# Attention over the batch: row statistics on ScalarE instead of VectorE, and PSUM places that swap by tile

## The chip, the cores and the metric

The kernel runs on one core of a Trainium2 chip. The metric is the device time of one execution in microseconds; an execution that is profiled on the hardware gives the profile. The core has five engines with a queue each: TensorE (PE; its weight loads are PEld) for matrix products, VectorE (DVE), ScalarE (ACT) and GpSimd (POOL) for elementwise work, and SyncE (SP), which here issues transfers. Each queue runs in order; engines wait for each other only by counting semaphores.

## The reference, cut to what matters

The input `x` is 4 x 2048 rows of 256 values. Two layers follow; each normalises the rows, makes an attention-like sum `s` and a gate `g` and adds `s * silu(g)` to `x`. The changed code is the end of the first layer and the attention of the second:

```python
x = x + s * g                                  # end of layer 0
xn = _layernorm(x)                             # (x - mean) / sqrt(var + 1e-5), per row
q, k, v = xn @ Wq.T + bq, xn @ Wk.T + bk, xn @ Wv.T + bv     # 16 heads of 16
scores[i, j] = q_i . k_j / 4                   # i, j over the batch of 4, causal
attn = exp(scores - max) / (1 + sum(exp))      # per row and head
s = sum over j of attn[i, j] * v_j
g = silu(mixture of 8 experts, top 2, of the same xn)
x = x + s * g
```

The first axis of `xn` is what the attention runs over, so each of the 2048 positions is a small problem of 4 x 4 scores in 16 heads, alone.

## The kernel before

The program has five stages one after the other: `prepare`, `mix` (layer 0), `attend` (the attention, L987), `experts`, `combine`. `attend` works in 16 tiles of 128 positions (partitions) by 4 batch rows of 256. Each engine has its own `body(i, u, left)` for tile `t = 2i + u`, `left` tiles still to come; what is done in one body belongs to several tiles, since the engines work ahead:

- **VectorE**, body `t`: `layer0_finish(t + 2)` (L270): the product with layer 0's output out of PSUM (L274), the sum that makes the new `x` of that tile (L277), and the rows' mean and variance, four `bn_stats` (L281) and four `bn_aggr` (L287). Then, for tile `t`: the ten products of queries and keys in four multiplies (L1177) of 1024, 768, 512 and 256 columns, their sums per head (L1183), maximum, difference (L1191), after ScalarE's exponentials the sum (L1195), the reciprocal, and the weights (L1201), which let GpSimd start.
- **GpSimd**, body `t`: waits for the weights, then weights times values for key `j = 0` to 3 (L1147) with a running sum for `j >= 1` (L1153). After `j = 1` it calls `row_factors(t + 3)` (L291): four operations on 128x4 that wait for the statistics (L294) and give the factor and the offset of the rows' normalisation. That call is left out for the last three tiles.
- **ScalarE**, body `t`, in this order: exponentials of `t` (L1363), the keys of `t + 1` out of PSUM, storing the logits of `t`, normalising the rows of `t + 2` (L1322) into `xn` (two buffers, also stored to DRAM from SyncE's queue), logits, values of `t + 1`, the turned rows of `t + 2` (L1351), logits again, queries of `t + 2`. The copies of queries, keys and values are all L1346.
- **TensorE**, body `t`: three products with bias (`qkv_product`, L313), for queries, keys and values; between them layer 0's output of tile `t + 2` (L265) and the gate's logits (L1420); then the turning of the rows of `t + 1` (L309) and of the logits. Queries and values use the PSUM tile `pY`, keys `pX`. Before the queries of a tile TensorE waits until the values before are out of `pY` (L1406) and both halves of the turned rows `xnT` are copied (L1407):

```python
pe.wait_ge(v_evac, t + 1)
pe.wait_ge(t_evac, KD * t + KD)
qkv_product(pe, v, 0, pY, q_done)
```

All waits are written by hand as counts; no planner orders the work. The statistics of tiles 0 and 1 are made before the loop, that of tile 2 in VectorE's body 0.

Of the kernel before, what the change touches and what calls it, by code (L numbers as in the profile page):

```python
# [19 lines left out]
P = 128  # L20
B, S, D = 4, 2048, 256
KD = D // P
# [202 lines left out]
def bridge(nc, v, at):  # L225

    def sb(name, shape, dt=F32):
        return at.enter_context(nc.sbuf_tensor(name, shape, dt))

    nx = v.next = Shared()  # L230
    nx.xnT = sb("c_xnT", [P, KD, BANK])
    nx.bias3 = sb("c_bias3", [P, 3 * D], BF16)
    nx.ones3 = sb("c_ones3", [P, P], BF16)
    nx.st = sb("c_st", [P, B, 6])
    nx.mv = sb("c_mv", [P, B, 2])
    nx.ta = sb("c_ta", [P, B])
    nx.tb = sb("c_tb", [P, B])
    nx.r1 = [sb(f"c_r1{n}", [P, B]) for n in range(2)]
    nx.nmr = [sb(f"c_nmr{n}", [P, B]) for n in range(2)]
    nx.mhalf = sb("c_mhalf", [P, B])  # L240
    nx.mone = sb("c_mone", [P, B])
    nx.eps = sb("c_eps", [P, B])
    nx.pT = at.enter_context(nc.psum_tensor("c_pT", [P, KD, BANK], F32))
    nx.pY = at.enter_context(nc.psum_tensor("c_pY", [P, B, D], F32))
    nx.open = v.sem("c_open")
# [12 lines left out]
    nx.q_done = v.sem("c_q_done")  # L258


def layer0_output(pe, v, t):
# [8 lines left out]
def layer0_finish(dve, v, t):  # L270

    nx = v.next
    dve.wait_ge(nx.o_done, t + 1)
    dve.tensor_tensor(v.prod_st[:, t, :], nx.pT[:, :, :].rearrange("p k c -> p (k c)"), v.prod_st[:, t, :],  # L274
                      ALU.mult).then_inc(nx.op_ready, 1)
    dve.wait_ge(nx.op_ready, t + 1)
    dve.tensor_tensor(v.x_st[:, :, t, :], v.prod_st[:, t, :].rearrange("p (b d) -> p b d", b=B),  # L277
                      v.x_st[:, :, t, :], ALU.add).then_inc(nx.x1_ready, 1)
    dve.wait_ge(nx.x1_ready, t + 1)
    for b in range(B):  # L280
        last = dve.bn_stats(nx.st[:, b, :], v.x_st[:, b, t, :])  # L281
    last.then_inc(nx.bn, 1)
    dve.wait_ge(nx.bn, t + 1)
    if t:
        dve.wait_ge(nx.r_ready, t)
    for b in range(B):
        last = dve.bn_aggr(nx.mv[:, b, :], nx.st[:, b, :])  # L287
    last.then_inc(nx.stats, 1)


def row_factors(pool, v, t):  # L291

    nx, u = v.next, t % 2
    pool.wait_ge(nx.stats, t + 1)  # L294
    pool.tensor_tensor(nx.ta[:, :], nx.mv[:, :, 1], nx.eps[:, :], ALU.add).then_inc(nx.rchain, 1)  # L295
    pool.tensor_tensor(nx.tb[:, :], nx.mv[:, :, 0], nx.mone[:, :], ALU.mult).then_inc(nx.rchain, 1)
    pool.wait_ge(nx.rchain, 3 * t + 2)
    if t >= 2:
        pool.wait_ge(nx.xn_ready, t - 1)
    pool.tensor_tensor(nx.r1[u][:, :], nx.ta[:, :], nx.mhalf[:, :], ALU.pow).then_inc(nx.rchain, 1)  # L300
    pool.wait_ge(nx.rchain, 3 * t + 3)
    pool.tensor_tensor(nx.nmr[u][:, :], nx.tb[:, :], nx.r1[u][:, :], ALU.mult).then_inc(nx.r_ready, 1)
# [7 lines left out]
        last.then_inc(v.next.t_done, 1)  # L310


def qkv_product(pe, v, n, dst, done):  # L313

    nx = v.next
    for m in range(2):
        pe.matmul(dst[:, 2 * m:2 * m + 2, :], nx.ones3[:, :],
                  nx.bias3[:, n * D:(n + 1) * D].unsqueeze(1).broadcast_to([P, 2, D]),
                  start=True, stop=False, skip_group_check=True)
    for kk in range(KD):  # L320
        for b in range(B):
            last = pe.matmul(dst[:, b, :], nx.xnT[:, kk, b * P:(b + 1) * P], v.wqkv[:, kk, n * D:(n + 1) * D],  # L322
                             start=False, stop=(kk == KD - 1), skip_group_check=True)
    last.then_inc(done, 1)
# [141 lines left out]
def mix(nc, v):  # L466
# [4 lines left out]
    with ExitStack() as c:  # L471
# [96 lines left out]
        with nc.Block() as block:  # L568
# [16 lines left out]
            def _(pool):  # L585
# [34 lines left out]
                pool.memset(nx.mhalf[:, :], -0.5).then_inc(nx.open, 1)  # L620
                pool.memset(nx.eps[:, :], EPS).then_inc(nx.open, 1)
                pool.memset(nx.mone[:, :], -1.0).then_inc(nx.open, 1)
                linked(pool.memset(nx.bias3[:, :], 0.0))
                linked(pool.memset(nx.ones3[:, :], 1.0))
                pool.wait_ge(v.late_in, 32)
# [11 lines left out]
                pool.wait_ge(nx.open, 3)  # L637
                row_factors(pool, v, 0)

            @block.vector  # L640
# [346 lines left out]
def attend(nc, v):  # L987
# [10 lines left out]
    with ExitStack() as c:  # L998
# [44 lines left out]
        ident16 = sb("d_ident", [P, P], BF16)  # L1043
        zero16 = found[:, 0:P // 2].bitcast(BF16)

        pX = psum("c_pX", [P, B, D])
# [45 lines left out]
        with nc.Block() as block:  # L1092
# [21 lines left out]
            def _(pool):  # L1114
# [4 lines left out]
                def body(i, u, left):  # L1119
# [3 lines left out]
                    if t == 1:  # L1123
                        pool.memset(within2[:, :, :], 1.0).then_inc(filled, 1)
                        pool.memset(zero16, 0.0).then_inc(consts_ready, 1)
                        pool.tensor_copy(ident16[:, :], ident).then_inc(consts_ready, 1)
# [11 lines left out]
                    for j in range(B):  # L1138
# [11 lines left out]
                        if j:  # L1150
# [1 line left out]
                            pool.sem_inc(passed, 1)  # L1152
                            pool.tensor_tensor(o, o, part, ALU.add).then_inc(pv_step, 1)  # L1153
                            n += 1
                        if j == 1 and left >= 3:
                            row_factors(pool, v, t + 3)

                tiles(pool, body)

# [150 lines left out]

            @block.scalar
            def _(act):
                for s in (v_evac,):
                    act.sem_inc(s, 1)

                def normalise(t, u, stores):
                    act.wait_ge(r_ready, t + 1)
                    act.sem_inc(passed, 1)
                    act.wait_ge(xn_out[u], 16 * stores + 16)
                    act.sem_inc(passed, 1)  # L1320
                    for b in range(B):
                        last = act.activation(xn[u][:, b, :], v.x_st[:, b, t, :], ACT.Identity,  # L1322
                                              scale=r1[u][:, b:b + 1], bias=nmr[u][:, b:b + 1])
                    last.then_inc(xn_ready, 1)

                def take_logits(t):
                    act.wait_ge(l_done, t + 1)
# [25 lines left out]
                def take_q(t, reused=True):  # L1353
                    if reused:
                        act.wait_ge(sm, SM * (t - 1) + 1)
                    take(q, pY, q_done, q_evac, t, scale=DK ** -0.5)

                def take_k(t):
                    take(k, pX, k_done, k_evac, t)

                def exponents(t):
                    act.wait_ge(ex_in, t + 1)
# [2 lines left out]
                def take_v(t, u, reused=True):  # L1365
                    if reused:
                        act.wait_ge(pv_step, steps_through(t - 2))
                    take(vv[u], pY, v_done, v_evac, t)

                take_q(0, reused=False)  # L1370
                take_k(0)
# [7 lines left out]
                def body(i, u, left):  # L1379
# [7 lines left out]
                        normalise(t + 2, u, i + 1)  # L1387
                    if left >= 1:
                        take_logits(t + 1)
                        take_v(t + 1, 1 - u)  # L1390
                    if left >= 2:
                        take_turned(t + 2)
                    if left >= 1:
                        put_logits(t + 1)
                    if left >= 2:
# [5 lines left out]
            def _(pe):  # L1401
                def body(i, u, left):

                    t = 2 * i + u
                    if t:
                        pe.wait_ge(v_evac, t + 1)  # L1406
                        pe.wait_ge(t_evac, KD * t + KD)  # L1407
                        qkv_product(pe, v, 0, pY, q_done)
                        if left >= 2:
                            layer0_output(pe, v, t + 2)  # L1410
                        pe.wait_ge(k_evac, t)
                    qkv_product(pe, v, 1, pX, k_done)
                    if t == 0:
                        pe.wait_ge(op_ready, 2)
                        layer0_output(pe, v, 2)
# [5 lines left out]
                                             xnT[:, kk, b * P:(b + 1) * P], start=(kk == 0), stop=(kk == KD - 1))  # L1421
                    last.then_inc(l_done, 1)
                    pe.wait_ge(q_evac, t + 1)
                    qkv_product(pe, v, 2, pY, v_done)
                    if left >= 1:
                        if left >= 2:
                            pe.wait_ge(op_ready, t + 3)
# [10 lines left out]
                for n in range(K2 // NB):  # L1438
                    pe.wait_ge(ohl_ready, n + 1)
                    pe.wait_ge(ohc_ready, n + 1)  # L1440
                    if n == 0:
                        pe.matmul(ptab, ident16[:, :], zero16, start=True, stop=False, skip_group_check=True)
# [5 lines left out]
                pe.matmul(ptab, ident16[:, :], zero16, start=False, stop=True,  # L1448
                          skip_group_check=True).then_inc(table, 1)


# [543 lines left out]
```

## Time and profile before

| | |
|---|---|
| median of 3 runs | 1339.4 us (1339.05 to 1341.31) |
| profiled execution | 1339.15 us, span 1337.4 us |
| mean granted TensorE clock | 0.947 of full speed |
| busy over the span | PE 1158.8 us (87%), VectorE 1010.5 (76%), GpSimd 643.8 (48%), ScalarE 624.1 (47%) |

The span is the time from the first to the last instruction of the profiled execution. Busy shares are means over five stages that are bound by different things; the attention loop takes about a sixth of the span, so it is read from windows and a timeline of its own tiles. A row of a timeline gives the start, the length, the engine, the source line, the operation, the tensors written and read with their shapes, a count if several alike were merged, and in brackets the idle time in front with what ended it.

### The profile page before, as it was taken

How to read it: one execution, taken by the hardware profiler on the slowest of the kernel's cores; microseconds unless marked ns; L12 is line 12 of the kernel's file. 1: busy time of each engine (PE TensorE's matmuls, PEld its weight loads, DVE VectorE, ACT ScalarE, POOL GpSimd, SP SyncE). 2: the span in 40 equal slices, each digit the busy share in tenths (PEclk: the TensorE clock that was granted, in tenths of full speed). 3: DMA queues.
4: the chain of work that ended last, by engine and by line, in shares of the span. 5: the costliest groups of instructions: out<-in, count | busy, mean ns of one | idle time of the engine just before them, and what ended most of it. 6: DMA issues, size and time to landing. Idle time of an engine off the chain costs nothing. (4 is left out here: it accounts for less than half of the span.)

```text
span 1337.4 us, 20503 instructions
## 1 busy us (share of the span) xinstructions
PE 1158.8 (87%) x7464; PEld 792.8 (59%) x7464; DVE 1010.5 (76%) x1924; ACT 624.1 (47%) x979; POOL 643.8 (48%) x624
## 2 busy tenths in 40 slices
PE   3799999999999993349999999999999999999910
PEld 3556655567777672225766667676676766667610
DVE  6767787789999999967686767767677676775538
ACT  4855655443444441026364453735536354463532
POOL 5860000158888887034456454554645546453310
PEclk9999999999999997559999999999999999999965
DMA  8180000011111120016446474564645546543259
GB/s 350 42 275 1 1 1 0 3 46 33 34 33 39 42 68 30 0 37 147 81 96 124 68 151 81 96 120 68 151 82 98 118 67 147 78 79 66 32 165 353
DMA packets 140532, 117.08 MB, mean 88 GB/s; under 512 B 81648, under 2 KB 125552, under 8 KB 140304
## 3 DMA queue, kind: packets, MB, share of 16 engines
q1 hardware_dynamic: 107072, 80.23, 19.7%
q0 software_dynamic: 24624, 34.23, 16.5%
q10 hardware_dynamic: 8736, 1.33, 0.5%
q8 instruction: 59, 0.97, 0.3%
q14 instruction: 41, 0.34, 0.1%
HBM read 55.19 MB, written 44.30 MB: 74 GB/s over the span
## 5 line engine op out<-in xcount | busy, mean ns | idle before, releaser
L1843 ACT ACTIVATE e_h_all<-e_pH,e_b1c,e_h_scale 128x512 f32<-128x512 f32 x256 | 199.8, 781 | 324.7 <-issue 244.9
L1915 PE MATMUL e_pY<-e_w_hi,e_h_hi 128*128 128x256 f16 x1024 | 279.3, 273 | 2.9 <-DVE late L1749 2.9
L1916 PE MATMUL e_pY<-e_w_lo,e_h_hi 128*128 128x256 f16 x1024 | 279.1, 273 | 0.0
L1917 PE MATMUL e_pY<-e_w_hi,late 128*128 128x256 f16 x1024 | 279.1, 273 | 0.0
L1625 POOL DMA_INDIRECT expert_sums<-late,e_dcol x128 | 212.7, 1662 | 100.2 <-DVE late L1789 65.7
L1603 POOL DMA_INDIRECT e_xg<-xn_rows,e_icol x124 | 140.1, 1130 | 241.5 <-DVE e_icol L1641 134.1
L1749 DVE TENSOR_TENSOR late<-e_h_all,e_h_hi 128x512 f16<-128x512 f32 x256 | 177.2, 692 | 34.9 <-ACT e_h_hi L1843 28.8
L1889 PE MATMUL e_pH<-e_xT,e_w_hi 128*128 128x512 f16 x512 | 195.4, 382 | 6.4 <-DVE e_w_lo L1693 2.5
L1891 PE MATMUL e_pH<-e_xT,e_w_lo 128*128 128x512 f16 x512 | 195.3, 381 | 0.0
L1890 PE MATMUL e_pH<-e_xT,e_w_hi 128*128 128x512 f16 x512 | 195.2, 381 | 0.0
L1785 DVE SCALAR_TENSOR_TENSOR late<-e_pY,e_y_scale,logit_st 128x512 f32<-128x512 f32 x64 | 48.1, 751 | 120.2 <-PE e_pY L1917 116.4
L322 PE MATMUL c_pY<-late,c_xnT 128*128 128x256 f32 x512 | 115.7, 379 | 0.0
L1915 PEld LDWEIGHTS e_pY<-e_w_hi,e_h_hi 128*128 128x128 f16 x1024 | 100.2, 98 | 20.0 <-DVE late L1749 5.2
L1916 PEld LDWEIGHTS e_pY<-e_w_lo,e_h_hi 128*128 128x128 f16 x1024 | 100.2, 98 | 14.9
L1917 PEld LDWEIGHTS e_pY<-e_w_hi,late 128*128 128x128 f16 x1024 | 100.2, 98 | 11.7
L322 PEld LDWEIGHTS c_pY<-late,c_xnT 128*128 128x128 f32 x512 | 97.2, 190 | 16.2
L295 POOL TENSOR_TENSOR c_ta<-c_mv,c_eps 128x4 f32<-128x4 f32 x16 | 17.7, 1106 | 174.7 <-DVE c_mv L287 174.7
L1843 ACT ACTIVATE e_h_hi<-e_pH,e_b1c,e_h_scale 128x512 f16<-128x512 f32 x128 | 99.2, 775 | 0.0
L1889 PEld LDWEIGHTS e_pH<-e_xT,e_w_hi 128*128 128x128 f16 x512 | 50.4, 98 | 65.2 <-PEq L1877 2.8
L1891 PEld LDWEIGHTS e_pH<-e_xT,e_w_lo 128*128 128x128 f16 x512 | 50.4, 98 | 61.2 <-issue 1.6
L1890 PEld LDWEIGHTS e_pH<-e_xT,e_w_hi 128*128 128x128 f16 x512 | 50.4, 98 | 56.7 <-issue 1.4
L1177 DVE TENSOR_TENSOR c_work<-c_work 128x1024 f32<-128x1024 f32 (+1 forms) x64 | 77.2, 1264 | 0.1
(266 smaller groups left out, 2160.4 us busy)
## 6 DMA issues: line engine op xcount, KB each, us to landing
shared<-expert_w SPq DMA_DIRECT2D x16, 1024.0 KB, 6.5
expert_sums<-logit_st SPq DMA_DIRECT2D x10, 1024.0 KB, 11.0
x_st<-x SPq DMA_DIRECT2D x16, 512.0 KB, 8.9
xn_rows<-shared SPq DMA_DIRECT2D x16, 512.0 KB, 3.0
f_ya<-expert_sums SPq DMA_DIRECT2D x16, 512.0 KB, 7.1
out<-x_st SPq DMA_DIRECT2D x8, 1024.0 KB, 8.2
e_xg<-xn_rows,e_icol POOLq DMA_INDIRECT x128, 2.8
expert_sums<-late,e_dcol POOLq DMA_INDIRECT x128, 3.9
```

The costliest lines, as they stand in the source:

```text
L322: last = pe.matmul(dst[:, b, :], nx.xnT[:, kk, b * P:(b + 1) * P], v.wqkv[:, kk, n * D:(n + 1) * D], start=False, stop=(kk == KD - 1), ski ...
L1177: last = dve.tensor_tensor(qk[:, PAIR0[j]:PAIR0[j] + w, :], q[:, j:B, :], spread(k[:, j, :], w), ALU.mult)
L1603: pool.indirect_dma_start(xg[:, q, 0:D + E], None, v.xn3_dram, bass.IndirectOffsetOnAxis(icol[u][:, q:q + 1], axis=0), bounds_check=N - 1, ...
L1625: pool.indirect_dma_start(v.y_dram, bass.IndirectOffsetOnAxis(dcol[u][:, q:q + 1], axis=0), yo[:, q, :], None, bounds_check=N + CAP - 1, o ...
L1749: dve.tensor_tensor(h_lo[:, h, :], h_all[h % 2][:, :], h_hi[:, h, :], ALU.subtract).then_inc(h_lo_ready, 1)
L1843: last = act.activation(dst, pH[h % NPH][:, :], ACT.Relu, bias=b1c[eu][:, h:h + 1], scale=h_scale[eu][:, 0:1])
L1889: pe.matmul(pH[h % NPH][:, :], w1_hi[:, k, rows], x_hi[:, k, :], start=(k == 0), stop=False)
L1890: pe.matmul(pH[h % NPH][:, :], w1_hi[:, k, rows], x_lo[:, k, :], start=False, stop=False)
L1891: last = pe.matmul(pH[h % NPH][:, :], w1_lo[:, k, rows], x_hi[:, k, :], start=False, stop=(k == KD - 1))
L1915: pe.matmul(pY[:, q, :], h_hi[:, h, cols], w2_hi[:, h, :], start=(h == 0), stop=False)
L1916: pe.matmul(pY[:, q, :], h_hi[:, h, cols], w2_lo[:, h, :], start=False, stop=False)
L1917: last = pe.matmul(pY[:, q, :], h_lo[:, h, cols], w2_hi[:, h, :], start=False, stop=(h == HT - 1))
```

## The change

For tiles 3 to 15 VectorE leaves `layer0_finish` after L277. ScalarE makes the statistics, with two functions in its body `t` for tile `t + 3`: `sums` copies the four rows' parts of `x` onto themselves with the sum accumulated, `squares` makes the mean (divided by 16, negative) and squares the rows less the mean with the sum accumulated. The squares themselves go into the free `xn` buffer and are not used. GpSimd's `row_factors` takes the results in these tiles, with 16 in place of -1 as the factor of the offset, and is called after the last `j` instead of after `j = 1`. Values move behind the turned rows in ScalarE's order. In even tiles queries and values stay in `pY` and keys in `pX`; in odd tiles it is the other way round, so that the queries' place is free once the keys before are out. `qkv_product` for the queries waits for each half of `xnT` before the half that needs it. A constant tile (16) is added and an identity tile shares another's place.

```diff
+    nx.total, nx.less, nx.vary = nx.st[:, :, 0], nx.mv[:, :, 0], nx.mv[:, :, 1]
+BY_DVE = 3
@@ layer0_finish
                       v.x_st[:, :, t, :], ALU.add).then_inc(nx.x1_ready, 1)
+    if t >= BY_DVE:
+        return
     dve.wait_ge(nx.x1_ready, t + 1)
     for b in range(B):
         last = dve.bn_stats(nx.st[:, b, :], v.x_st[:, b, t, :])
@@ row_factors
+    if t < BY_DVE:
...
+    else:
+        pool.tensor_tensor(nx.ta[:, :], nx.vary, nx.eps[:, :], ALU.add).then_inc(nx.rchain, 1)
+        pool.tensor_tensor(nx.tb[:, :], nx.less, nx.sixteen[:, :], ALU.mult).then_inc(nx.rchain, 1)
@@ qkv_product
+        if tile is not None:
+            pe.wait_ge(nx.t_evac, KD * tile + kk + 1)
@@ attend, gpsimd
-                        if j == 1 and left >= 3:
-                            row_factors(pool, v, t + 3)
+                    if left >= 3:
+                        row_factors(pool, v, t + 3)
@@ attend, scalar
+                def sums(t):
+                    act.wait_ge(nx.x1_ready, t + 1)
+                    act.wait_ge(r_ready, t)
+                    for b in range(B):
+                        last = act.activation(v.x_st[:, b, t, :], v.x_st[:, b, t, :], ACT.Identity, accum_out=nx.total[:, b:b + 1])
+                    last.then_inc(nx.summed, 1)
+                def squares(t):
+                    act.wait_ge(nx.summed, t - BY_DVE + 1)
+                    act.activation(nx.less, nx.total, ACT.Copy, scale=-1.0 / (16 * D)).then_inc(nx.centred, 1)
+                    act.wait_ge(nx.centred, t - BY_DVE + 1)
+                    act.wait_ge(xn_out[t % 2], 16 * (t // 2) + 16)
+                    for b in range(B):
+                        last = act.activation(xn[t % 2][:, b, :], v.x_st[:, b, t, :], ACT.Square, bias=nx.less[:, b:b + 1],
+                                              scale=1.0 / 16, accum_out=nx.vary[:, b:b + 1])
+                    last.then_inc(nx.stats, 1)
...
-                    take(q, pY, q_done, q_evac, t, scale=DK ** -0.5)
+                    take(q, (pY, pX)[t % 2], q_done, q_evac, t, scale=DK ** -0.5)
...
                         take_logits(t + 1)
-                        take_v(t + 1, 1 - u)
+                    if left >= 3:
+                        sums(t + 3)
                     if left >= 2:
                         take_turned(t + 2)
+                    if left >= 1:
+                        take_v(t + 1, 1 - u)
+                    if left >= 3:
+                        squares(t + 3)
@@ attend, tensor
+                    one, other = (pY, pX) if t % 2 == 0 else (pX, pY)
                     if t:
-                        pe.wait_ge(v_evac, t + 1)
-                        pe.wait_ge(t_evac, KD * t + KD)
-                        qkv_product(pe, v, 0, pY, q_done)
+                        pe.wait_ge(k_evac, t)
+                        qkv_product(pe, v, 0, one, q_done, t)
                         if left >= 2:
                             layer0_output(pe, v, t + 2)
-                        pe.wait_ge(k_evac, t)
-                    qkv_product(pe, v, 1, pX, k_done)
+                        pe.wait_ge(v_evac, t)
+                    qkv_product(pe, v, 1, other, k_done)
...
-                    qkv_product(pe, v, 2, pY, v_done)
+                    qkv_product(pe, v, 2, one, v_done)
```

## Rows read from the trace of the kernel before

**Rows 1.** Windows, one tile: window, its length, busy time by engine (instructions), clock, DMA.
```profile
477.41:493.32 15.91, 14.64 (x99) 11.65 (x98) 15.15 (x23) 7.58 (x13) 12.90 (x11) 1.00 0.12 37
```

**Rows 2.** Timeline of VectorE, one middle tile: start, length (us), instruction, gap before.
```profile
365.51 0.42 DVE L1201 TENSOR_TENSOR c_att<-c_ex,c_mx 128x256 f32<-128x256 f32 x1
...
367.11 1.93 DVE L277 TENSOR_TENSOR x_st<-prod_st,x_st 128x1024 f32<-128x1024 f32 x1
369.07 1.41 DVE L281 BATCH_NORM_STATS2 c_st<-x_st 128x6 f32<-128x256 f32 x4
...
370.80 4.47 DVE L1177 TENSOR_TENSOR c_work<-c_work 128x1024 f32<-128x1024 f32 x4
...
378.96 0.67 DVE L1191 TENSOR_TENSOR c_ex<-c_sc,c_mx 128x256 f32<-128x256 f32 x1
```

**Rows 3.** The same view, the end of the first tile.
```profile
285.89 0.42 DVE L1201 TENSOR_TENSOR c_att<-c_ex,c_mx 128x256 f32<-128x256 f32 x1
```

**Rows 4.** The same view, the loop's end.
```profile
492.90 0.42 DVE L1201 TENSOR_TENSOR c_att<-c_ex,c_mx 128x256 f32<-128x256 f32 x1
493.47 8.54 DVE L1177 TENSOR_TENSOR c_work<-c_work 128x1024 f32<-128x1024 f32 x4
...
508.30 7.67 DVE L1177 TENSOR_TENSOR c_work<-c_work 128x1024 f32<-128x1024 f32 x4
```

**Rows 5.** Timeline of ScalarE, the same tile.
```profile
367.23 2.06 ACT L1322 ACTIVATE shared<-x_st,c_nmr,c_r 128x256 f32<-128x256 f32 x4
...
370.94 1.03 ACT L1346 ACTIVATE c_v<-c_pY 128x1024 f32<-128x1024 f32 x1 [1.49 <-PE c_pY L322]
...
379.66 0.42 ACT L1363 ACTIVATE c_ex<-c_ex 128x256 f32<-128x256 f32 x1 [1.41 <-DVE c_ex L1191]
```

**Rows 6.** Timeline of TensorE, the same tile.
```profile
373.08 0.59 PE L317 MATMUL c_pY<-c_bias,c_ones 128*128 128x512 bf16 x2 [1.26 <-ACT c_xnT L1351]
```

**Rows 7.** Timeline of GpSimd, the same tile.
```profile
366.02 1.93 POOL L1147 TENSOR_TENSOR prod_st<-c_att,c_v 128x1024 f32<-128x1024 f32 x1 [1.70 <-DVE c_att L1201]
368.13 2.26 POOL L1147 TENSOR_TENSOR c_pv<-c_att,c_v 128x768 f32<-128x768 f32 x1 [0.18 <-POOL prod_st L1147]
370.57 1.81 POOL L1153 TENSOR_TENSOR prod_st<-prod_st,c_pv 128x768 f32<-128x768 f32 x1 [0.18 <-POOL c_pv L1147]
372.34 1.19 POOL L295 TENSOR_TENSOR c_ta<-c_mv,c_eps 128x4 f32<-128x4 f32 x1
...
376.04 1.06 POOL L1147 TENSOR_TENSOR c_pv<-c_att,c_v 128x512 f32<-128x512 f32 x1
...
379.53 0.72 POOL L1153 TENSOR_TENSOR prod_st<-prod_st,c_pv 128x256 f32<-128x256 f32 x1 [0.18 <-POOL c_pv L1147]
```

**Rows 8.** Timeline of VectorE, the first tile's multiplies, GpSimd having no product.
```profile
275.22 3.00 DVE L1177 TENSOR_TENSOR c_work<-c_work 128x1024 f32<-128x1024 f32 x4
```

**Rows 9.** Timeline of GpSimd, the stretch of Rows 4.
```profile
493.41 1.94 POOL L1147 TENSOR_TENSOR prod_st<-c_att,c_v 128x1024 f32<-128x1024 f32 x1 [1.69 <-DVE c_att L1201]
495.52 2.26 POOL L1147 TENSOR_TENSOR c_pv<-c_att,c_v 128x768 f32<-128x768 f32 x1 [0.18 <-POOL prod_st L1147]
497.96 2.31 POOL L1153 TENSOR_TENSOR prod_st<-prod_st,c_pv 128x768 f32<-128x768 f32 x1 [0.18 <-POOL c_pv L1147]
500.44 1.28 POOL L1147 TENSOR_TENSOR c_pv<-c_att,c_v 128x512 f32<-128x512 f32 x1 [0.18 <-POOL prod_st L1153]
```

**Rows 10.** Groups by shape of line L1177, 493.4 to 502.04 us: count, busy us, mean ns.
```profile
L1177 DVE TENSOR_TENSOR c_work<-c_work 128x1024 f32<-128x1024 f32 x1 | 3.0, 2956 | 0.1
L1177 DVE TENSOR_TENSOR c_work<-c_work 128x512 f32<-128x512 f32 x1 | 2.3, 2297 | 0.0
L1177 DVE TENSOR_TENSOR c_work<-c_work 128x768 f32<-128x768 f32 x1 | 2.2, 2246 | 0.0
L1177 DVE TENSOR_TENSOR c_work<-c_work 128x256 f32<-128x256 f32 x1 | 1.3, 1275 | 0.0
```

**Rows 11.** Timeline of ScalarE, the only table load in the loop.
```profile
282.82 1.28 ACT L1363 ACT_TABLE_LOAD   x1
```

More of the change, by code:

```diff
@@ L244, in bridge @@
     nx.pY = at.enter_context(nc.psum_tensor("c_pY", [P, B, D], F32))
+    nx.total, nx.less, nx.vary = nx.st[:, :, 0], nx.mv[:, :, 0], nx.mv[:, :, 1]
+    nx.sixteen = sb("c_sixteen", [P, B])
+    nx.summed = v.sem("c_summed")
+    nx.centred = v.sem("c_centred")
     nx.open = v.sem("c_open")
@@ L294, in row_factors @@
     pool.wait_ge(nx.stats, t + 1)
-    pool.tensor_tensor(nx.ta[:, :], nx.mv[:, :, 1], nx.eps[:, :], ALU.add).then_inc(nx.rchain, 1)
-    pool.tensor_tensor(nx.tb[:, :], nx.mv[:, :, 0], nx.mone[:, :], ALU.mult).then_inc(nx.rchain, 1)
+    if t < BY_DVE:
+        pool.tensor_tensor(nx.ta[:, :], nx.mv[:, :, 1], nx.eps[:, :], ALU.add).then_inc(nx.rchain, 1)
+        pool.tensor_tensor(nx.tb[:, :], nx.mv[:, :, 0], nx.mone[:, :], ALU.mult).then_inc(nx.rchain, 1)
+    else:
+        pool.tensor_tensor(nx.ta[:, :], nx.vary, nx.eps[:, :], ALU.add).then_inc(nx.rchain, 1)
+        pool.tensor_tensor(nx.tb[:, :], nx.less, nx.sixteen[:, :], ALU.mult).then_inc(nx.rchain, 1)
     pool.wait_ge(nx.rchain, 3 * t + 2)
@@ L310, in turn_rows, with qkv_product @@
         last.then_inc(v.next.t_done, 1)
-def qkv_product(pe, v, n, dst, done):
+def qkv_product(pe, v, n, dst, done, tile=None):
     nx = v.next
@@ L622, in _ @@
                 pool.memset(nx.mone[:, :], -1.0).then_inc(nx.open, 1)
+                pool.memset(nx.sixteen[:, :], 16.0).then_inc(nx.open, 1)
                 linked(pool.memset(nx.bias3[:, :], 0.0))
@@ L636, in _ @@
                 pool.sem_inc(nx.bias_ready, 1)
-                pool.wait_ge(nx.open, 3)
+                pool.wait_ge(nx.open, 4)
                 row_factors(pool, v, 0)
@@ L1042, in attend @@
         empty = sb("d_empty", [P, P])
-        ident16 = sb("d_ident", [P, P], BF16)
+        ident16 = empty[:, 0:P // 2].bitcast(BF16)
         zero16 = found[:, 0:P // 2].bitcast(BF16)
@@ L1125, in body @@
                         pool.memset(zero16, 0.0).then_inc(consts_ready, 1)
-                        pool.tensor_copy(ident16[:, :], ident).then_inc(consts_ready, 1)
+                        pool.tensor_copy(ident16, ident).then_inc(consts_ready, 1)
                         pool.tensor_copy(code[:, :], v.cst[:, C_G:C_G + K2]).then_inc(consts_ready, 1)
@@ L1312, in _ @@
             def _(act):
-                for s in (v_evac,):
-                    act.sem_inc(s, 1)
                 def normalise(t, u, stores):
@@ L1355, in take_q @@
                         act.wait_ge(sm, SM * (t - 1) + 1)
-                    take(q, pY, q_done, q_evac, t, scale=DK ** -0.5)
+                    take(q, (pY, pX)[t % 2], q_done, q_evac, t, scale=DK ** -0.5)
                 def take_k(t):
-                    take(k, pX, k_done, k_evac, t)
+                    take(k, (pX, pY)[t % 2], k_done, k_evac, t)
                 def exponents(t):
@@ L1367, in take_v @@
                         act.wait_ge(pv_step, steps_through(t - 2))
-                    take(vv[u], pY, v_done, v_evac, t)
+                    take(vv[u], (pY, pX)[t % 2], v_done, v_evac, t)
                 take_q(0, reused=False)
@@ L1441, in _ @@
                     if n == 0:
-                        pe.matmul(ptab, ident16[:, :], zero16, start=True, stop=False, skip_group_check=True)
+                        pe.matmul(ptab, ident16, zero16, start=True, stop=False, skip_group_check=True)
                     for a in range(WIDE):
@@ L1447, in _ @@
                     last.then_inc(used[n % 2], 1)
-                pe.matmul(ptab, ident16[:, :], zero16, start=False, stop=True,
+                pe.matmul(ptab, ident16, zero16, start=False, stop=True,
                           skip_group_check=True).then_inc(table, 1)
```

## The prediction

> **What bounds the kernel now.** I read the page's slices for the stage in which the edited code runs (the attention loop of 16 tiles), then the windows of busy time, then the timeline of one middle tile for VectorE, GpSimd, TensorE and ScalarE, and last the timeline of the loop's end. In a window of one tile's length, 15.91 us, TensorE is busy 14.64, VectorE 15.15, GpSimd 12.90 and ScalarE 7.58, all at the granted clock 1.00 [rows 1]: two engines stand near full, and one has to ask which one closes its loop without waiting for another.
>
> I count a tile from the end of the instruction that writes the attention weights (L1201) to the next such end. That end is 365.51 + 0.42 = 365.93 in the tile shown; I call it A [rows 2]. The first is 285.89 + 0.42 = 286.31 and the fourteenth 492.90 + 0.42 = 493.32, so 13 tiles take 207.0 us, 15.92 each [rows 3, 4].
>
> VectorE's tile is a chain of its own: L277 to 369.04, the statistics L281 and L287, the multiplies L1177 from 370.80 to 375.27, reductions and softmax, with no gap in front of them [rows 2]; ScalarE waits 1.41 us for VectorE before the exponentials, not the other way round [rows 5]. TensorE's tile has one gap: 1.26 us in which the bias product for the queries waits for ScalarE's copy of the turned rows [rows 6]; 14.64 + 1.26 = 15.90. So the two loops tie, and a change must shorten both to gain.
>
> What matters most is inside VectorE's tile. L277 starts at 367.11 while GpSimd's product L1147 runs until 366.02 + 1.93 = 367.95; it ends 1.09 after that, at 369.04. GpSimd's next product starts at 368.13 and ends at 370.39, that is 1.35 after L277's end, though it is shorter than the one before it. L1177's first multiply starts at 370.80 and GpSimd's sum L1153 ends at 370.57 + 1.81 = 372.38 [rows 2, 7]. Alone, all four multiplies take 3.00 us [rows 8]; here they take 4.47. So a two-input VectorE instruction and a GpSimd one run one after the other. The Trainium skill, SBUF — State Buffer, section "SBUF: two separate sides", says so as a rule: the pair of ports that both engines share is held for a whole instruction and the other side blocks; the trace agrees (the 1.09 and 1.35 us above). By sharing without a lock the change would gain (the faster rival below); by the lock it loses.
>
> **The change part by part.**
>
> *Statistics off VectorE (tiles 3 to 15, so the 13 intervals above).* Gone: four L281 (1.41 us together) and four L287. Between L277's end, 369.04, and L1177's start, 370.80, that is 1.76 us [rows 2]. But L281 has one input and GpSimd worked beside it; what moves up into this place is L1177, with two.
>
> *The row factors move from the middle to the end of GpSimd's tile.* Now, after its second product and sum, GpSimd turns to the four small operations of `row_factors`, from 372.34 to 376.04 [rows 7]. During this time L1177 runs nearly undisturbed and is over (375.27) when GpSimd's next large product begins. Afterwards GpSimd goes straight on, product, sum, product, sum. The trace has this case: at the loop's end there are no row factors, and the multiplies that took 4.47 take 8.54 [rows 4]. There, each of GpSimd's operations ends before a multiply does and the other way round: GpSimd's ends are 495.35, 497.78, 500.27, 501.72 [rows 9], the multiplies' ends (durations in [rows 10], each starting about 0.08 before the one in front ends) 496.43, 498.59, 500.81, 502.01. Steps: 1.08 for the multiply of 1024, product 1.35, multiply of 768 0.81, sum 1.68, multiply of 512 0.54, product 0.91, multiply of 256 0.29.
>
> Put together for a tile after the change, in us from A: L277 ends at 3.10 and GpSimd's second product at 4.46, as now [rows 2, 7]. Multiply of 1024, waiting since 3.1: 4.46 + 1.08 = 5.54. Sum of 768: + 1.68 = 7.22. Multiply of 768: + 0.81 = 8.03. Product of 512: + 0.91 = 8.94. Multiply of 512: + 0.54 = 9.48. Sum of 512: some 1.27 alone, an estimate midway between 1.81 for 768 and 0.72 for 256 [rows 7], of which 0.15 has gone by while it waits: + 1.12 = 10.60. Multiply of 256: + 0.29 = 10.89. Now it is 375.27 - 365.93 = 9.34. So the reductions start 1.55 later, not 1.76 earlier. What follows is unchanged but for L1191: it takes 0.67 beside GpSimd's last sum (379.53), and would take 0.42, as L1201 of the same size does [rows 2, 7], since GpSimd, with two more operations of about 0.72, is done with its sums at some 12.4 from A and L1191 comes at 14.5. That gives back 0.25. Net +1.30 a tile, period 17.22.
>
> Bounds of this term: if the last pair doesn't collide (the multiply of 256 goes before the sum of 512 and ends at some 9.8 instead of 10.89), +0.2; if the collisions also hit L1191, +1.55.
>
> *ScalarE's new work.* Eight activations of 128x256 with an accumulated output and one of 128x4. The trace has no accumulating one; the nearest row is L1322, four activations of 128x256 in 2.06 [rows 5]. Lower bound 2 x 2.06 + 0.2 = 4.3; upper bound, if each read of a sum costs as much again as one of L1322's four (2.06 / 4, about 0.5), 8.3. I take 5.5, near the row. ScalarE's 7.58 becomes 13.1, below 17.2. Order matters more: `sums` waits for L277 (A + 3.1), then the turned rows are copied, values, `squares`, logits, queries. With 2.5 us each, sums end at 5.7, turned rows and values, 1.03 or little more each [rows 5], at 7.8, squares 10.7, queries at the earliest after L1177 (10.89), so 11.9; the exponentials come about 2.2 before the next A, as now, at 15.0. Three us of cover; it is gone if an accumulation costs over half a microsecond extra. The wait in `sums` has the turned rows' copy queued behind it, and that holds TensorE's queries; TensorE, with 14.64 us of work in 17.2, can bear it. The statistics reach GpSimd at 10.7, before it ends its sums at 12.4, so its wait for them holds nothing up; at most 3.7 us of row factors [rows 7] then end at 16.1, before the next A at 17.2. Were they later than that, the next tile's first product would queue behind them. No transfer is moved: the store of `xn` whose buffer `squares` overwrites was issued a tile before.
>
> *The PSUM places swap.* Queries of a tile no longer wait for the copy of the values before, and each half of the product waits for its half of the turned rows. This can take away TensorE's 1.26 us [rows 6]; its tile could be 14.64. VectorE's is 17.2, so it is worth nothing in the middle; TensorE then waits for ScalarE's copy, which stands behind `sums`. Late next is VectorE itself.
>
> *The loop's end.* The multiplies of the last tile but one start at 493.47, when GpSimd's product has just started (493.41), and take 8.54; those of the last take 7.67 [rows 4, 9]. With TensorE ahead the keys are there earlier, and the first of the two should go like the second, VectorE getting the ports first: an estimate of -1.0, for which 0 is the other end. One constant more, one identity tile placed elsewhere: nothing, off every path.
>
> Sum: 13 x 1.30 = 16.9, less 1.0, = +15.9. The profiled execution lasted 1339.15 (span 1337.4), the median is 1339.4, 0.25 more: 1339.4 + 15.9, about 1355. Its own range, with ScalarE's cost and a tenth or two per tile: 1349 to 1361.
>
> **Rivals.**
> (1) Faster: VectorE keeps the shared ports for its four multiplies in a row. They would end at 4.46 + 3.00 = 7.46 instead of 9.34; with L1191 VectorE's tile is 13.8, and TensorE bounds at 14.64: 13 x (14.64 - 15.91) = -16.5, 1323. For it: the multiplies stand back to back in VectorE's queue; against it: in [rows 9, 10] GpSimd got its turn after each multiply. Decisive is who gets the ports when a multiply ends.
> (2) No change: the last pair doesn't collide, 13 x 0.2 - 1.0 = +1.6, 1341. For it: these are the shortest instructions; against: GpSimd waits only 0.18 between two operations, and a multiply of 512 covers that.
> (3) Slower still: ScalarE's new functions and the exponentials need different tables, a load before the exponentials in every tile, 1.28 us [rows 11], on VectorE's path: 15.9 + 13 x 1.28, 1372. An accumulation that costs over 0.5 us ends near the same place. For it: nothing in the trace shows a Square. Against: copies, scalings and exponentials follow each other with one load in the whole loop. The Trainium skill, ScalarE: Activation LUTs, section "Table sets: the hidden batching unit", says that the cheap functions are in every set, without naming Square there; no run here shows it.
>
> **Chances.** Forecast 0.72, (1) 0.14, (2) 0.06, (3) 0.08. A difference within 0.2% (2.7 us) can't be told from none. So faster 0.14, within 0.06, slower 0.80. The range takes in the upper half of what ScalarE may cost and the lower bound's neighbourhood: 1345 to 1369.
>
> **What would show it.** The period from L1201 to L1201 near 17.2 (the 14.64 of TensorE: rival 1); L1177's four multiplies some 7.7 us a tile; GpSimd's operations and the multiplies ending in turn; the row factors after the last sum; TensorE's wait longer, not gone; ScalarE waiting for VectorE before the exponentials. The prediction is wrong if multiplies end without GpSimd in between, if VectorE waits for the exponentials by more than 0.5 us, or if GpSimd's first product of a tile starts well after L1201.

## The result and the profile after

The changed kernel takes 1356.72 us (median of 4 runs, 1355.96 to 1356.98), against 1340.36 (1339.05 to 1342.67) for the kernel before on the same chip: ratio 1.0123, 95% interval 1.0111 to 1.0135. That is 16.4 us slower; 15.9 was forecast. The profiled execution took 1356.94 us (span 1355.2). In the changed kernel L1201 has become L1217, L277 is L284, L1177 is L1193, L1191 is L1207, and GpSimd's product and sum are L1163 and L1169.

First the windows, one middle tile from weights to weights: window, its length, busy time of PE, PEld, DVE, ACT and POOL, granted clock, DMA.

```profile
389.61:406.90 17.29, 14.75 (x85) 11.08 (x84) 16.60 (x16) 10.32 (x31) 12.69 (x11) 1.00 0.10 32
```

VectorE is busy longer than in [rows 1], 16.60 us instead of 15.15, although its statistics are gone. TensorE has the same work, 14.75 us, and now waits. ScalarE's 10.32 us hold the new work. The window of [rows 1] is no good measure of it, because it lies near the loop's end and holds the copy of the keys (L1346) of two tiles; a stretch of 16.00 us from the middle of the loop before shows 6.68 us, not 7.58:

```profile
374.00:390.00 16.00, 14.73 (x85) 11.28 (x84) 15.24 (x24) 6.68 (x12) 13.25 (x12) 1.00 0.11 34
```

The timeline of VectorE for the changed kernel's tile, with the end of the first tile above it:

```profile
285.92 0.42 DVE L1217 TENSOR_TENSOR c_att<-c_ex,c_mx 128x256 f32<-128x256 f32 x1
...
389.61 0.43 DVE L1217 TENSOR_TENSOR c_att<-c_ex,c_mx 128x256 f32<-128x256 f32 x1
...
391.20 1.93 DVE L284 TENSOR_TENSOR x_st<-prod_st,x_st 128x1024 f32<-128x1024 f32 x1
393.05 7.87 DVE L1193 TENSOR_TENSOR c_work<-c_work 128x1024 f32<-128x1024 f32 x4
...
404.65 0.43 DVE L1207 TENSOR_TENSOR c_ex<-c_sc,c_mx 128x256 f32<-128x256 f32 x1
405.56 0.72 DVE L1211 TENSOR_REDUCE c_mx<-c_ex 128x64 f32<-128x320 f32 x1 [0.48 <-ACT c_ex L1395]
...
406.90 0.42 DVE L1217 TENSOR_TENSOR c_att<-c_ex,c_mx 128x256 f32<-128x256 f32 x1
```

The period: from 285.92 + 0.42 to the fourteenth such end (510.94, below) it is 224.60 / 13 = 17.28 us, before 15.92 [rows 3, 4]. The multiplies come directly after L284, and take 7.87 us where they took 4.47 [rows 2]. They end at 400.92, that is A + 10.88 with A = 390.04 (before: A + 9.34). Two more views of the same stretch: the multiplies by shape (count, busy us, mean ns, idle before), and the timeline of GpSimd.

```profile
L1193 DVE TENSOR_TENSOR c_work<-c_work 128x768 f32<-128x768 f32 x1 | 2.6, 2566 | 0.0
L1193 DVE TENSOR_TENSOR c_work<-c_work 128x1024 f32<-128x1024 f32 x1 | 2.5, 2511 | 0.0
...
L1193 DVE TENSOR_TENSOR c_work<-c_work 128x512 f32<-128x512 f32 x1 | 1.5, 1544 | 0.0
L1193 DVE TENSOR_TENSOR c_work<-c_work 128x256 f32<-128x256 f32 x1 | 1.5, 1483 | 0.0
```

```profile
392.23 2.25 POOL L1163 TENSOR_TENSOR c_pv<-c_att,c_v 128x768 f32<-128x768 f32 x1 [0.18 <-POOL prod_st L1163]
394.66 2.58 POOL L1169 TENSOR_TENSOR prod_st<-prod_st,c_pv 128x768 f32<-128x768 f32 x1 [0.18 <-POOL c_pv L1163]
397.41 1.55 POOL L1163 TENSOR_TENSOR c_pv<-c_att,c_v 128x512 f32<-128x512 f32 x1 [0.18 <-POOL prod_st L1169]
399.15 1.49 POOL L1169 TENSOR_TENSOR prod_st<-prod_st,c_pv 128x512 f32<-128x512 f32 x1 [0.18 <-POOL c_pv L1163]
400.82 0.62 POOL L1163 TENSOR_TENSOR c_pv<-c_att,c_v 128x256 f32<-128x256 f32 x1 [0.18 <-POOL prod_st L1169]
...
402.30 0.20 POOL L308 TENSOR_TENSOR c_ta<-c_mv,c_eps 128x4 f32<-128x4 f32 x1
...
403.83 0.20 POOL L315 TENSOR_TENSOR c_nmr<-c_tb,c_r 128x4 f32<-128x4 f32 x1
```

Taken together (each multiply starts some 0.08 us before the one in front ends, since the four durations add up to 8.10 and the group lasts 7.87), ends in us from A, beside the ones that the prediction worked out:

| ends | predicted | measured |
|---|---|---|
| GpSimd product 768 | 4.46 | 4.44 |
| multiply 1024 | 5.54 | 5.52 |
| GpSimd sum 768 | 7.22 | 7.20 |
| multiply 768 | 8.03 | 8.01 |
| GpSimd product 512 | 8.94 | 8.92 |
| multiply 512 | 9.48 | 9.48 |
| GpSimd sum 512 | 10.60 | 10.60 |
| multiply 256 | 10.89 | 10.88 |

The two engines end an instruction in strict turn. After the last sum GpSimd makes the row factors undisturbed, 402.30 to 404.03, and then waits for the next weights. The timelines of ScalarE and TensorE:

```profile
393.16 0.42 ACT L1344 ACTIVATE x_st<-x_st 128x256 f32<-128x256 f32 x1 [1.89 <-DVE x_st L284]
393.48 0.19 ACT L1344 ACTIVATION_READ_ACCUMULATOR x_st<-x_st 128x1 f32 x1
...
394.77 1.06 ACT L1383 ACTIVATE c_xnT<-c_pT 128x512 f32<-128x512 f32 x2
...
396.87 0.51 ACT L1354 ACTIVATE shared<-x_st,c_mv 128x256 f32<-128x256 f32 x1
...
398.76 0.19 ACT L1354 ACTIVATION_READ_ACCUMULATOR shared<-x_st,c_mv 128x1 f32 x1
...
400.96 1.02 ACT L1378 ACTIVATE c_work<-c_pY 128x1024 f32<-128x1024 f32 x1 [1.93 <-DVE c_work L1193]
405.11 0.42 ACT L1395 ACTIVATE c_ex<-c_ex 128x256 f32<-128x256 f32 x1 [3.12 <-DVE c_ex L1207]
```

```profile
395.40 3.72 PE L337 MATMUL c_pY<-late,c_xnT 128*128 128x256 f32 x16 [2.54 <-ACT c_xnT L1383]
```

ScalarE's row L1344 writes a row part in 0.40 us, and a separate read of the accumulator follows. The statistics are done at 398.76 + 0.19 = 398.95, A + 8.9. ScalarE then waits for VectorE's multiplies (1.93) and for its softmax (3.12); VectorE's only wait in the tile is the 0.48 for the exponentials. TensorE's gap before the queries is 2.54 us where it was 1.26 [rows 6]: 14.75 + 2.54 = 17.29, the tile. Last the loop's end, on VectorE:

```profile
510.52 0.42 DVE L1217 TENSOR_TENSOR c_att<-c_ex,c_mx 128x256 f32<-128x256 f32 x1
510.86 7.68 DVE L1193 TENSOR_TENSOR c_work<-c_work 128x1024 f32<-128x1024 f32 x4
...
525.09 7.66 DVE L1193 TENSOR_TENSOR c_work<-c_work 128x1024 f32<-128x1024 f32 x4
...
538.92 0.42 DVE L1217 TENSOR_TENSOR c_att<-c_ex,c_mx 128x256 f32<-128x256 f32 x1
```

From A of the fourteenth tile to A of the last: 510.94 to 539.34, 28.40 us. Before it was 29.24. So the loop ends 16.78 us later, 13 x (17.28 - 15.92) - 0.84 with unrounded periods. The two profiled spans differ by 17.8; the further 1.0 us comes after the loop, and I did not follow it: the runs of one kernel differ by as much.

### The profile page after: what moved, and what is told of

The parts are those of the page before. It is cut to its first block and busy times, and to the rows that moved or that the text cites. A ratio compares the mean times of both kernels' runs of the same rounds, so it can differ in the third digit from the quotient of the medians.

```text
span 1355.2 us, 20618 instructions
## 1 busy us (share of the span) xinstructions
PE 1166.4 (86%) x7464; PEld 795.5 (59%) x7464; DVE 1028.8 (76%) x1820; ACT 671.2 (50%) x1200; POOL 639.6 (47%) x625
## 3 DMA queue, kind: packets, MB, share of 16 engines
q10 hardware_dynamic: 8736, 1.33, 0.5%
## 5 line engine op out<-in xcount | busy, mean ns | idle before, releaser
L1193 DVE TENSOR_TENSOR c_work<-c_work 128x1024 f32<-128x1024 f32 (+1 forms) x64 | 120.7, 1944 | 0.0
L337 PE MATMUL c_pX<-late,c_xnT 128*128 128x256 f32 x384 | 92.5, 396 | 14.4 <-ACT c_xnT L1383 14.4
L337 PE MATMUL c_pY<-late,c_xnT 128*128 128x256 f32 x384 | 88.7, 385 | 10.1 <-ACT c_xnT L1383 10.1
L337 PEld LDWEIGHTS c_pX<-late,c_xnT 128*128 128x128 f32 x384 | 75.8, 199 | 30.4 <-ACT c_xnT L1383 17.8
L1926 PEld LDWEIGHTS e_pH<-e_xT,e_w_hi 128*128 128x128 f16 x512 | 50.3, 98 | 65.5 <-DMA e_xT<-e_xs 2.9
L337 PEld LDWEIGHTS c_pY<-late,c_xnT 128*128 128x128 f32 x384 | 73.5, 193 | 25.0 <-ACT c_xnT L1383 13.2
```

The costliest lines, as they stand in the source:

```text
L1193: last = dve.tensor_tensor(qk[:, PAIR0[j]:PAIR0[j] + w, :], q[:, j:B, :], spread(k[:, j, :], w), ALU.mult)
L1926: pe.matmul(pH[h % NPH][:, :], w1_hi[:, k, rows], x_hi[:, k, :], start=(k == 0), stop=False)
```

## The experiments

The theory on trial: the edit that costs the time is the place of the row factors. In the middle of GpSimd's tile they kept that engine's large operations away from VectorE's multiplies; at the end they don't. Rivals: ScalarE's new work, and the PSUM swap. Ratios are against runs of the kernel before on the same chip, with 95% intervals. Three switches make most of the kernels that were run; their ratios in one table:

| statistics on | swap | factors last | after j = 1 | after j = 0 |
|---|---|---|---|---|
| VectorE | no | 1.0194 | 1 (before) | 1.0003 |
| VectorE | yes | 1.0207 | 0.9981 | 0.9867 |
| ScalarE | yes | 1.0123 (the change) | 0.9982 | 0.9903 |
| ScalarE | no | 1.0133 | | |

**Row factors back in the middle of the changed kernel.**

```diff
+                        if j == 1 and left >= 3:
+                            row_factors(pool, v, t + 3)
-                    if left >= 3:
-                        row_factors(pool, v, t + 3)
```

> The changed kernel with row_factors back behind j = 1 in GpSimd's tile; all else as changed. Theory L (the place of row_factors decides, because a two-input VectorE instruction and a GpSimd one run one after the other): GpSimd waits there for the statistics until about 8.9 us from A, VectorE's multiplies of 768, 512 and 256 run without it and end at 9.0 instead of 10.9 us; L1191 then meets GpSimd's sum of 512 (about +0.5); tile 15.9 us instead of 17.3, time 1339 us (1335 to 1343). Rival S (ScalarE's statistics lengthen the tile, by the copy of the turned rows standing behind the sums): ScalarE's and TensorE's queues are untouched, so the tile stays 17.3 us and the time 1357 us.

Measured: 1336.57 us, 0.9982 [0.9969, 0.9996]. With this one call moved back, the loss of 1.2% is gone. VectorE, then GpSimd, in one tile:

```profile
384.18 5.94 DVE L1193 TENSOR_TENSOR c_work<-c_work 128x1024 f32<-128x1024 f32 x4
```

```profile
390.16 0.20 POOL L308 TENSOR_TENSOR c_ta<-c_mv,c_eps 128x4 f32<-128x4 f32 x1 [1.79 <-ACT shared L1354]
```

GpSimd waits 1.79 us for ScalarE's squares, and meanwhile the last multiplies run without it: the four take 5.94 instead of 7.87 and end 8.96 us after A (9.0 expected). The tile is 15.74.

**The same move alone, in the kernel before.**

```diff
-                        if j == 1 and left >= 3:
-                            row_factors(pool, v, t + 3)
+                    if left >= 3:
+                        row_factors(pool, v, t + 3)
```

> The kernel before with one edit: row_factors moved behind the last j. Statistics stay on VectorE, PSUM places as before. Theory L: the multiply of 1024 still waits for GpSimd's first sum and ends 7.5 us from A, then multiplies and GpSimd's operations take turns, the multiply of 256 ends at about 11.6 instead of 9.3 us; tile 17.9 us, time 1366 us (1358 to 1369), slower than the whole change. Rival S: ScalarE does nothing new, so 1340 us.

Measured: 1366.09 us, 1.0194 [1.0177, 1.0212]. VectorE and GpSimd:

```profile
382.43 6.81 DVE L1177 TENSOR_TENSOR c_work<-c_work 128x1024 f32<-128x1024 f32 x4
```

```profile
384.18 1.82 POOL L1147 TENSOR_TENSOR c_pv<-c_att,c_v 128x512 f32<-128x512 f32 x1 [0.18 <-POOL prod_st L1153]
...
389.82 0.21 POOL L295 TENSOR_TENSOR c_ta<-c_mv,c_eps 128x4 f32<-128x4 f32 x1
```

Two lines that add and remove no instruction cost 26 us, more than the whole change. The multiplies take 6.81 instead of 4.47, and GpSimd's product of 512 columns takes 1.82 instead of 1.06 [rows 7].

**The swap alone, in the kernel before** (PSUM places, half waits, values' copy behind the turned rows).

```diff
-                    take(q, pY, q_done, q_evac, t, scale=DK ** -0.5)
+                    take(q, (pY, pX)[t % 2], q_done, q_evac, t, scale=DK ** -0.5)
...
-                        pe.wait_ge(v_evac, t + 1)
-                        pe.wait_ge(t_evac, KD * t + KD)
-                        qkv_product(pe, v, 0, pY, q_done)
+                        pe.wait_ge(k_evac, t)
+                        qkv_product(pe, v, 0, one, q_done, t)
```

> The kernel before with the PSUM places swapped by tile, the values' copy behind the turned rows and the wait for each half of them; statistics and row_factors as before. Theory L (VectorE's chain sets the tile): TensorE's 1.26 us wait gets no one anything; tile 15.9 us, the end of the loop about 1 us shorter: 1339 us (1337 to 1341). Rival P (TensorE's loop sets the tile of the kernel before): tile 14.7 us, 1323 us.

Measured: 1337.50 us, 0.9981 [0.9972, 0.9991]. The wait before the queries is gone, and TensorE waits just as long at another place, where the row's releaser is VectorE's product out of PSUM:

```profile
381.79 1.07 PE L309 MATMUL c_pT<-cst,shared 128*128 128x128 f32 x8 [1.24 <-DVE prod_st L274]
```

The two loops did tie: freeing one leaves the other at 15.93 a tile. What the swap gains, some 2 us, lies outside the 13 tiles: the first tile ends 1.33 us earlier and the last two take 28.42 instead of 29.24.

**The two missing sides of the change.** The changed kernel with the statistics left on VectorE; this is the kernel with the swap alone, and

```diff
-                        if j == 1 and left >= 3:
-                            row_factors(pool, v, t + 3)
+                    if left >= 3:
+                        row_factors(pool, v, t + 3)
```

And the changed kernel without the swap:

```diff
-                    take(q, (pY, pX)[t % 2], q_done, q_evac, t, scale=DK ** -0.5)
+                    take(q, pY, q_done, q_evac, t, scale=DK ** -0.5)
...
-                        pe.wait_ge(k_evac, t)
-                        qkv_product(pe, v, 0, one, q_done, t)
+                        pe.wait_ge(v_evac, t)
+                        pe.wait_ge(nx.t_evac, KD * t + KD)
+                        qkv_product(pe, v, 0, pY, q_done)
```

> The kernel before with the swap of the PSUM places, the half waits and the values' copy behind the turned rows, and the row factors at the end of GpSimd's tile; only the statistics stay on VectorE. It differs from the changed kernel by the statistics alone. Theory (VectorE's chain alone bounds a tile once the factors stand last, so the swap is worth nothing there but at the loop's end): tile 18.04 as with the factors alone (1366.1), loop's end about -0.8 us: 1365, between 1362 and 1368. Rival (the 9.4 us by which the changed kernel is below that one come from the swap): 1357, tile 17.3.

> The changed kernel without the swap: queries and values in one PSUM place, keys in the other, in every tile, and the old waits before the queries; the order of ScalarE's work stays as changed, so the queries wait for the values' copy behind the turned rows. Theory (VectorE's multiplies bound the tile, TensorE has slack): tile 17.28 unchanged, TensorE's wait before the queries moves to the values' copy, some 1.0 us later; time 1357, between 1355 and 1360. Rival (TensorE's loop decides, its wait of 2.54 us grows by the 1.0 us of the values' copy): 13 x 1.0 more, 1370.

Measured: 1366.19 us, 1.0207 [1.0190, 1.0224], and 1356.95 us, 1.0133 [1.0116, 1.0150]. So with the row factors last the swap is worth nothing (1366.09 and 1366.19; 1356.95 and 1356.72), and the move of the statistics to ScalarE gains 9.5 us by the medians (0.84% by the ratios). TensorE's rows, of the first and of the second kernel:

```profile
394.74 1.06 PE L309 MATMUL c_pT<-cst,shared 128*128 128x128 f32 x8 [1.68 <-DVE prod_st L274]
```

```profile
397.30 0.61 PE L330 MATMUL c_pY<-c_bias,c_ones 128*128 128x512 bf16 x2 [1.55 <-ACT c_v L1378]
```

In both TensorE waits, for VectorE's chain in the first, for the copy of the values in the second; the tiles stay at 18.04 and 17.25.

**GpSimd's products cut**, to part the collisions from ScalarE's work, which stays whole.

```diff
...
+                        if j:
+                            w = hh = 1
...
```

> The changed kernel, but GpSimd's products and sums for the keys j = 1 to 3 are cut to 16 columns each (the weighted sum for these keys is left out but for one head of one query); the number of instructions, waits and the place of row_factors stay, VectorE's and ScalarE's work too. Theory L: L284 still waits for the product of j = 0, the four multiplies then take 3.0 us instead of 7.9; VectorE's tile would be 12.5, TensorE's loop bounds near 14.9: 1356.7 - 13 x 2.4 less some 5 to 9 at the loop's end, 1318 us (1312 to 1327). Rival S (ScalarE's new work behind which the turned rows wait): nothing of it is changed, 1355 us.

Measured: 1309.70 us, 0.9775 [0.9751, 0.9799]; right in direction, but 8 us below the value expected and below its range. VectorE, GpSimd, and the window of one tile:

```profile
375.13 3.10 DVE L1200 TENSOR_TENSOR c_work<-c_work 128x1024 f32<-128x1024 f32 x4
```

```profile
375.46 0.97 POOL L1176 TENSOR_TENSOR prod_st<-prod_st,c_pv 128x16 f32<-128x16 f32 x1 [0.18 <-POOL c_pv L1170]
...
378.52 0.22 POOL L1176 TENSOR_TENSOR prod_st<-prod_st,c_pv 128x16 f32<-128x16 f32 x1 [0.18 <-POOL c_pv L1170]
...
383.27 0.20 POOL L308 TENSOR_TENSOR c_ta<-c_mv,c_eps 128x4 f32<-128x4 f32 x1 [4.52 <-ACT shared L1361]
```

```profile
371.69:386.17 14.48, 14.48 (x85) 11.17 (x84) 11.79 (x15) 10.32 (x29) 7.05 (x11) 1.00 0.13 39
```

With GpSimd's long instructions gone the multiplies are back at 3.10 and TensorE is busy for the whole tile, with all of ScalarE's 10.32 us in place. So ScalarE's work is not what the change pays for. GpSimd shows the same turns from its side: a sum of 16 columns takes 0.97 beside the multiplies and 0.22 alone. Most of the miss is in the 13 tiles, which are 37.7 us shorter where 31.2 were expected: with TensorE never waiting a tile takes 14.48, not 14.9. The last two tiles take 24.6 instead of 28.4, and the profiled spans differ by 47.0, so the rest comes after the loop.

**Row factors first, after j = 0, in the changed kernel.**

```diff
-                    if left >= 3:
-                        row_factors(pool, v, t + 3)
+                        if j == 0 and left >= 3:
+                            row_factors(pool, v, t + 3)
```

> The changed kernel with row_factors behind j = 0, so that GpSimd stands still from about 2 us to the statistics at 8.9 us from A. Theory L: the four multiplies run alone, 3.0 us, end at 6.1 instead of 10.9 us from A; VectorE's tile could be 12.5 us, TensorE's 14.7 then bounds: 1324 us if GpSimd's later sums stay clear of the next tile's multiplies, up to 1345 us if they run into them. Rival S: 1357 us or more, since GpSimd's waiting is added.

Measured: 1326.43 us, 0.9903 [0.9887, 0.9920]. VectorE, GpSimd, ScalarE:

```profile
392.86 5.91 DVE L1193 TENSOR_TENSOR c_work<-c_work 128x1024 f32<-128x1024 f32 x4
```

```profile
401.83 0.20 POOL L308 TENSOR_TENSOR c_ta<-c_mv,c_eps 128x4 f32<-128x4 f32 x1 [1.27 <-ACT shared L1354]
```

```profile
398.52 1.02 ACT L1378 ACTIVATE c_v<-c_pY 128x1024 f32<-128x1024 f32 x1 [2.89 <-POOL prod_st L1169]
```

The time is in the range, but the multiplies were expected to run alone in 3.0 us, and they still collide (5.91): GpSimd's products and sums for the other keys now stand beside them. GpSimd no longer waits for VectorE, since its product for j = 0 runs later in the tile; it waits for the squares, which stand behind the values' copy, which waits for GpSimd's own last sum.

**The squares ahead of the values' copy**, in that kernel, to shorten this ring.

```diff
+                    if left >= 3:
+                        squares(t + 3)
                     if left >= 1:
                         take_v(t + 1, 1 - u)
-                    if left >= 3:
-                        squares(t + 3)
```

> The kernel with row_factors behind j = 0, and squares put before the values' copy in ScalarE's order. In e4 GpSimd's tile (15.15 us) has one gap, 1.27 us for the statistics, and these stand behind the values' copy, which waits 2.89 us for GpSimd's last sum of the tile before: a loop of GpSimd and ScalarE. Theory L with that loop: the gap goes, TensorE's loop (14.7 to 14.9) bounds: 1326.4 - 13 x 0.3 = 1322 us (1319 to 1325). If the gap was not in the bounding loop: 1326 us.

Measured: 1334.91 us, 0.9957 [0.9942, 0.9972]: a miss, slower than without the edit (a tile of 15.64 instead of 15.15). VectorE and GpSimd:

```profile
391.82 2.06 DVE L1207 TENSOR_TENSOR c_ex<-c_sc,c_mx 128x256 f32<-128x256 f32 x1
```

```profile
388.43 0.20 POOL L308 TENSOR_TENSOR c_ta<-c_mv,c_eps 128x4 f32<-128x4 f32 x1 [3.21 <-ACT shared L1354]
...
391.80 1.80 POOL L1169 TENSOR_TENSOR prod_st<-prod_st,c_pv 128x768 f32<-128x768 f32 x1 [0.18 <-POOL c_pv L1163]
```

The ring was not the bound. GpSimd now stands elsewhere against VectorE: it waits longer (3.21), the multiplies are shorter (4.76), but its sum of 768 begins at 391.80, 0.02 us ahead of VectorE's difference, which takes 2.06 instead of 0.43. I priced the ring and left out that its length sets which instructions meet.

**The place after j = 0 with the statistics left on VectorE, with and without the swap.**

```diff
-                        if j == 1 and left >= 3:
+                        if j == 0 and left >= 3:
                             row_factors(pool, v, t + 3)
```

> The kernel before with the PSUM places swapped (as e3) and row_factors behind j = 0; statistics stay on VectorE. If the gain of e4 (1326 us) comes from the place of row_factors and from TensorE's freed loop together, and not from the statistics' move: multiplies start at 4.9 us from A, end alone near 7.9, VectorE's tile 14.4 plus what it meets of GpSimd's later sums, TensorE's 14.5; tile 14.5 to 15.3, 1320 to 1331 us. If the statistics' move carries e4's gain: 1337 us as e3.

> The kernel before with one edit: row_factors behind j = 0. VectorE's multiplies run alone as in e7, but TensorE's loop with its 1.26 us wait for the values' and the turned rows' copies stays as it was, 15.9 us. If the two loops tie in the kernel before: 1339 us (1336 to 1342), no change. If VectorE's chain alone sets the tile: 1320 to 1331 us as e7.

Measured: 1321.93 us, 0.9867 [0.9851, 0.9884], and 1340.53 us, 1.0003 [0.9992, 1.0013]. The first beats both kernels. Its VectorE, GpSimd and window:

```profile
391.25 1.41 DVE L281 BATCH_NORM_STATS2 c_st<-x_st 128x6 f32<-128x256 f32 x4
...
392.98 3.00 DVE L1179 TENSOR_TENSOR c_work<-c_work 128x1024 f32<-128x1024 f32 x4
```

```profile
390.09 2.91 POOL L1149 TENSOR_TENSOR prod_st<-c_att,c_v 128x1024 f32<-128x1024 f32 x1
393.15 1.09 POOL L295 TENSOR_TENSOR c_ta<-c_mv,c_eps 128x4 f32<-128x4 f32 x1
```

```profile
387.82:402.33 14.51, 14.51 (x91) 11.17 (x83) 13.75 (x23) 6.70 (x13) 13.32 (x12) 1.00 0.12 38
```

The four statistics have one input, and GpSimd's product of 1024 columns, which ends 1.79 us after L277's end (391.21), runs out beside them, at 393.00. When the multiplies start at 392.98, GpSimd turns to four small operations, and the multiplies take 3.00. TensorE is busy for the whole tile. Without the swap the multiplies take 3.00 as well, but TensorE keeps its wait, the tiles take 15.60, 15.88 and 16.21 in turn, and nothing is gained:

```profile
389.11 0.59 PE L317 MATMUL c_pY<-c_bias,c_ones 128*128 128x512 bf16 x2 [1.27 <-ACT c_xnT L1351]
```

The swap alone gave 0.19% and the early place alone nothing; together they give 1.33%, as expected where two loops tie.

## Why the prediction was right

*What bounds the kernel.* That TensorE's and VectorE's loops tie is shown by the swap alone and the early place alone, of which each frees one loop and leaves the tile at 15.93 and at 15.9 on average, and by both together, 14.50. One reading in it is wrong: VectorE's chain is not without a gap. Between the difference and the sum it waits for ScalarE's exponentials, before as after the change:

```profile
380.11 0.71 DVE L1195 TENSOR_REDUCE c_mx<-c_ex 128x64 f32<-128x320 f32 x1 [0.48 <-ACT c_ex L1363]
```

The 0.48 us are the same in both kernels, so the forecast of the difference did not suffer.

*Statistics off VectorE.* The prediction gave this step no price of its own; it expected the multiplies to move up into a meeting with GpSimd, priced that together with the next step, and the sum of the two was right. Measured by itself the step gains 9.5 us with the factors last (18.04 against 17.28 a tile); with them in the middle it makes no difference that can be told (0.9981 and 0.9982), and with them first it loses 0.4%.

*Row factors to the end.* This is the step that costs: 19 us by the changed kernel with and without it, 26 by the kernel before. The chain of eight ends held to 0.02 us. It could be worked out because the loop's end of the kernel before had shown the same meeting [rows 4, 9, 10]. Reductions start 1.54 later (1.55 predicted), L1207 takes 0.43 (0.42), the tile grows by 1.36 (1.30).

*Who holds the ports.* The measured turns are what the faster rival denied: VectorE's four multiplies stand back to back in its queue, and GpSimd still gets in after each. So the two engines wait for each other here without any semaphore. The Trainium skill, SBUF — State Buffer, section "SBUF: two separate sides", tells of an exclusive hold for one instruction; the trace agrees, GpSimd's sum of 768, issued at 394.66 during a multiply that ends at 395.56, ends 1.68 after that end. When both had an instruction waiting, the other engine was always next: the eight ends of the table alternate. (The prediction's sentence on sharing without a lock does not fit its faster rival, in which VectorE holds the ports for four instructions; the measured turns exclude both.)

*ScalarE's new work.* The term that was mis-sized: 5.5 us taken, 10.32 - 6.68 = 3.64 measured, which is below even the lower bound of 4.3 taken from L1322, and the statistics were ready at A + 8.9, not 10.7 (the prediction's own terms, 3.1 + 2.5 + 2.1 + 2.5 + 0.2, give 10.4). An accumulating activation takes 0.40 to 0.49 us from start to start, less than L1322's half microsecond [rows 5]. ScalarE's path had slack: 3.12 us in front of the exponentials (some three were worked out), so the wrong size did not reach the time. No table was loaded in a tile, against the third rival: the loop's timeline of ScalarE has one load, in its first tile, as before.

*PSUM places.* "Worth nothing in the middle": shown by the kernel without the swap, 1356.95 against 1356.72. TensorE's wait grew to 2.54, as said.

*The loop's end.* -1.0 predicted, -0.84 measured: the first of the two tiles' multiplies takes 7.68 instead of 8.54, the second 7.66. The prediction put this beside the swap, but the kernel without the swap ends in the same 28.40 us, so here the swap is not needed for it. That TensorE's slack in the longer tile does it instead is not shown by itself.

## What to carry to other kernels

Where two-input instructions of VectorE and instructions of GpSimd run at once, draw up who follows whom: a chain of short or one-input work on one engine is a cover for the other, and to move it can cost more than the work that the move saves. When two engines' loops tie, test the edits together: each alone may show next to nothing (here 0.19% and none). Taking work off the busiest engine says little if what moves up into its place meets another engine.

## What was not expected of the hardware

Small GpSimd instructions lose most from the turns for their size: a sum of 16 columns takes 0.97 us beside a multiply and 0.22 alone. VectorE's product that reads PSUM (L274 before, L281 after) took 1.21 to 1.22 us in every kernel, also beside GpSimd's product of 1024 columns, while the sum behind it was held up (1.93 us). ScalarE's read of an accumulated sum is an instruction of its own of 0.19 us, half hidden beside the next activation (starts 0.40 apart for copies, 0.49 with a bias per row).
